# Moving z to token rows off TensorE: VectorE block transposes and sixteen SBUF-to-SBUF DMAs per sequence in a retention block plus expert layer

## The reference

```python
def block(h, p):
    r = _retention(h, wk)                  # scores q k^T, causal, divided by a row norm and a row sum, times v
    m = r @ w1 + b1
    a, gate = jnp.split(m, 2, axis=-1)
    m = a * jax.nn.silu(gate) @ w2 + b2    # "out projection"
    m = _groupnorm1(m, gg, gb)             # over a whole sequence
    y = m + h
    f = jax.nn.gelu(y @ wf1 + bf1_, approximate=False) @ wf2 + bf2_
    return (_layernorm(f + y, lg, lb), None)   # z = f + y; mean and variance over the 256 features of a token
out, _ = jax.lax.scan(block, x, params)    # 4 layers
x = _layernorm(x + out); x = _layernorm(x + _L0_ffn_ref(x, ...))   # 8 experts, hidden width 1024
```

## Time and profile before

| | |
|---|---|
| median of 3 runs | 2432.38 us (2432.0 to 2432.49) |
| the profiled execution, its own time | 2433.66 us |
| its span in the trace | 2431.9 us |
| TensorE busy | 2403.9 us, 99% of the span |
| VectorE / ScalarE / GpSimd busy | 1547.7 (64%) / 1366.8 (56%) / 1357.4 (56%) us |
| granted TensorE clock, mean | 0.996 of full |

### The profile page before, as it was taken

One profiled execution on the slowest core, in us unless ns is written; L12 is line 12 of the kernel. 1 busy time (PEld: TensorE's weight loads), 2 busy tenths in 40 slices (PEclk: granted clock), 3 DMA queues, 4 the chain that ended last, 5 costly groups with the idle time before them and its releaser, 6 DMA issues. The chain is left out here.

```text
span 2431.9 us, 35189 instructions
## 1 busy us (share of the span) xinstructions
PE 2403.9 (99%) x11662; PEld 2010.3 (83%) x11662; DVE 1547.7 (64%) x2876; ACT 1366.8 (56%) x2402; POOL 1357.4 (56%) x1255
## 2 busy tenths in 40 slices
PE   8999999999999999999999999999999999999998
PEld 6888888888888888887888888888888888888886
DVE  3566666666666666768787856665646756464545
ACT  4666766667666666666655644444444444444443
POOL 2355654455544644667888955546645556554444
PEclk9999999999999999999999999999999999999999
DMA  7011121111100112127655554544445443444442
GB/s 249 29 52 43 35 78 35 34 35 36 62 23 26 36 44 70 36 83 237 237 196 191 195 207 156 186 152 149 148 169 186 160 152 138 156 155 169 152 161 74
DMA packets 106823, 287.64 MB, mean 118 GB/s; under 512 B 7361, under 2 KB 77249, under 8 KB 90305
## 3 DMA queue, kind: packets, MB, share of 16 engines
q1 hardware_dynamic: 106128, 285.69, 33.7%
q10 hardware_dynamic: 560, 0.30, 0.0%
HBM read 216.36 MB, written 69.60 MB: 118 GB/s over the span
## 5 line engine op out<-in xcount | busy, mean ns | idle before, releaser
L701 POOL TENSOR_TENSOR hid_lo<-full,hid_hi 128x512 fp32r<-128x512 f32 x384 | 505.1, 1330 | 513.6 <-ACT full L1000 461.4
L1496 DVE SCALAR_TENSOR_TENSOR full<-ps,bias_cols,sum 128x512 f32<-128x512 f32 x384 | 288.2, 750 | 217.2 <-PE ps L1777 198.4
L1775 PE MATMUL ps<-hid_hi,m_w 128*128 128x512 f32 x1024 | 401.8, 392 | 0.1
L1777 PE MATMUL ps<-hid_hi,m_w 128*128 128x512 f32 x1024 | 398.8, 389 | 0.0
L1776 PE MATMUL ps<-hid_lo,m_w 128*128 128x512 f32 x1024 | 398.5, 389 | 0.0
L997 ACT ACTIVATE hid_hi<-ps,bias_cols 128x512 fp32r<-128x512 f32 x128 | 88.3, 690 | 496.4 <-PE ps L1777 496.4
L1775 PE MATMUL ps<-te_hi,m_w 128*128 128x512 f32 x896 | 351.5, 392 | 1.8 <-DVE sum L1483 0.9
L1777 PE MATMUL ps<-te_hi,m_w 128*128 128x512 f32 x896 | 349.3, 390 | 0.0
L1776 PE MATMUL ps<-te_lo,m_w 128*128 128x512 f32 x896 | 348.9, 389 | 0.0
L1777 PEld LDWEIGHTS ps<-hid_hi,m_w 128*128 128x128 f32 x1024 | 192.2, 188 | 40.4
L1775 PEld LDWEIGHTS ps<-hid_hi,m_w 128*128 128x128 f32 x1024 | 192.3, 188 | 39.5 <-issue 0.5
(11 more groups left out here) (210 smaller groups left out, 5593.2 us busy)
## 6 DMA issues: line engine op xcount, KB each, us to landing
m_w<-prepared SPq DMA_DIRECT2D x96, 1408.0 KB, 5.9
prepared<-m_w SPq DMA_DIRECT2D x32, 1408.0 KB, 5.8
h_store<-h_out SPq DMA_DIRECT2D x32, 512.0 KB, 3.2
we_raw<-in_W SPq DMA_DIRECT2D x64, 256.0 KB, 6.4
gate_bc<-gate_rows SPq DMA_DIRECT2D x64, 256.0 KB, 6.2
h_in<-h_store SPq DMA_DIRECT2D x24, 512.0 KB, 4.3
hT_in<-in_xT SPq DMA_DIRECT2D x8, 512.0 KB, 3.7
h_in<-in_x SPq DMA_DIRECT2D x8, 512.0 KB, 4.9
```

The source lines that it names most:

```text
L701: nc.gpsimd.tensor_tensor(out=hid_lo[:, k, :], in0=full[:, k, :], in1=f32(hid_hi[:, k, :]), op=ALU.subtract).then_inc(hid_ready, 1)
L1496: nc.vector.scalar_tensor_tensor(out=full[:, k, :], in0=src, scalar=b1_col(e, 2 * fp + BLOCK_ROW[k]), in1=other[:, :], op0=ALU.add, op1=AL ...
L1775: nc.tensor.matmul(out, w[0], x[0], start=first, stop=False, skip_group_check=True)
L1777: return nc.tensor.matmul(out, w[1], x[0], start=False, stop=last, skip_group_check=True)
```

## The change

For the first 15 steps' `z` (30 sequences) the eight PE transposes and the two ACT copies go. In their place:

- DVE turns each chunk of `z` by 32x32 blocks with `nc.vector.transpose` (`turn_z`) into the first half of the slot's `tmp` tile: four calls a step. Slot A's two stand inside `gated_products(B_, before)`, after each `gated`; slot B's first stands after `residual(B_, before, 0)`, its second inside `groupnorm_out(A_, now)`, ahead of `low_y` of chunk 0.
- SP then issues sixteen DMAs a sequence (`move_z`), each from a quadrant of 32 partitions of `tmp` to one of `z`: 32 rows x 8 pieces x 32 numbers, that is 32 KB in 256 pieces of 128 bytes. They stand ahead of the next loads of `h` for slot A, and between the loads and the store for slot B. `load_h` waits for its store first.
- `layernorm_stats` waits for all sixteen (`z_moved`), and so does the next `gated` of the slot, which overwrites `tmp`. Slot B's stats and var now stand after the two `divide(B_)`.
- `out_projection` goes over the input chunk `k` outside and the output chunk `c` inside, so that it needs the second chunk of its operand after six matmuls in place of three.
- `scores(B_)` goes chunk by chunk: blocks 0, 2, 3 with chunk 0, then block 0 with chunk 1, block 1, and blocks 2, 3 with chunk 1. Blocks 2 and 3 wait for the residuals that read their banks, no longer for `keep_z`.

The last step's two `z` keep the PE transposes. The core of the diff (renamed semaphores and the ends left out):

```diff
+        def turned_z(s):
+            return tmp[s][:, 0:DC, :].rearrange("p c n -> p (c n)").rearrange("p (r n b) -> p r n b", r=P // BLOCK, b=BLOCK)
+
+        def z_blocks(s, q, r):
+            rows = z[s][r * BLOCK:(r + 1) * BLOCK, :, :].rearrange("p k (c q b) -> p q (k c) b", c=DC, b=BLOCK)
+            return rows[:, q]
...
+            def move_z(s, it):
+
+                sp.wait_ge(h_new[s], it * U + U)
+                sp.wait_ge(z_ready[s], it * U + U)
+                for q in range(P // BLOCK):
+                    for r in range(P // BLOCK):
+                        sp.dma_start(z_blocks(s, q, r), turned_z(s)[q * BLOCK:(q + 1) * BLOCK, r, :, :]).then_inc(z_moved[s], DMA)
...
+                move_z(A_, it - 1)
+                load_next(A_)
+                move_z(B_, it - 1)
+                finish(A_)
+                load_next(B_)
+                finish(B_)
...
+            move_z(A_, STEPS - 2)
             sp.wait_ge(m2_psum[A_], DONE)
             load_weights(0)
             sp.wait_ge(y_ready[A_], DONE)
             load_weights(1)
+            move_z(B_, STEPS - 2)
             store_h(A_, STEPS - 2)
...
             def gated(s, at, c):
+                if c == 0:
+                    dve.wait_ge(z_moved[s], at.it * Z_MOVE + Z_STORE)
...
+            def turn_z(s, at, c):
+
+                dve.wait_ge(z_ready[s], at.base + residuals(s, c))
+                nc.vector.transpose(turned_z(s).rearrange("p r (k c) b -> p c k r b", c=DC)[:, c],
+                                    y[s][:, c, :].rearrange("p (k r b) -> p k r b", r=P // BLOCK, b=BLOCK)).then_inc(z_ready[s], 1)
...
-                    gated_products(B_, before)
+                    gated_products(B_, before, lambda part: turn_z(A_, before, part))
...
                     residual(B_, before, 0)
+                    turn_z(B_, before, 0)
...
-                groupnorm_out(A_, now)
+                groupnorm_out(A_, now, lambda part: before and part == 0 and turn_z(B_, before, 1))
                 low_p(B_, now, range(TB))
+                for half in range(2):
+                    divide(B_, now, half)
                 if before:
                     for blocks in HALVES:
                         layernorm_stats(B_, before, blocks)
                     layernorm_var(B_, before)
-                for half in range(2):
-                    divide(B_, now, half)
...
+            def scores_by_chunk(s, at, before):
+
+                for b in (0, 2, 3):
+                    score(s, at, b, 0, before)
+                score(s, at, 0, 1, before)
+                scores(s, at, (1,), before)
+                for b in (2, 3):
+                    score(s, at, b, 1, before)
...
-                for c in range(DC):
-                    for k in range(DC):
-                        pe.wait_ge(u_lo[s], at.base + 2 * k + 2)
+                for k in range(DC):
+                    pe.wait_ge(u_lo[s], at.base + 2 * k + 2)
+                    for c in range(DC):
                         ins = mm3(bank(s, OUT[c]), both(w, ALL, k, cols(c)), both(tu_sp[s], ALL, k), k == 0, k == DC - 1)
...
                 for c in range(DC):
                     project_t(A_, now, c)
                 if before:
-                    transpose_z(A_, before)
                     out_projection(B_, before)
...
                 group_moments(A_, now)
-                if before:
-                    transpose_z(B_, before)
-                else:
+                if not before:
                     pe.wait_ge(fold_out, 3 * (L - 1))
-                scores(B_, now, range(TB))
+                scores_by_chunk(B_, now, before)
```

More of the change, by code:

```diff
@@ L28 @@
 P = 128
+BLOCK = 32
 EPS = 1e-5
@@ L917, in hidden, with keep_z_end @@
                     high_f(s, at, c - 1)
-            def keep_z(s, at):
-                act.wait_ge(h_new[s], at.base + U)
+            def keep_z_end(s):
+                if s == A_:
+                    act.wait_ge(h_new[A_], LAST_STEP.base + U)
+                at_z, first = (z[A_], 0) if s == A_ else (z_end, 2)
                 for i in range(2):
[L922 to L930, removed]
+                    act.wait_ge(zT_psum, U * s + 2 * i + 2)
+                    nc.scalar.activation(at_z[:, 2 * i:2 * i + 2, :].rearrange("p k d -> p (k d)"), bank(s, first + i),
+                                         ACT.Copy).then_inc(z_kept, 2)
             def normalise_z(s, at, at_z=None):
@@ L1078, in body @@
                 high_t(B_, now)
-                if before:
-                    keep_z(B_, before)
-                else:
+                if not before:
                     act.wait_ge(fold_stored, (L - 1) * DMA)
@@ L1836, in project_t, with score, scores @@
                 ins.then_inc(t_psum[s], 2)
-            def scores(s, at, blocks):
+            def score(s, at, b, k, before):
+                q = slice(LO[b], S)
+                if k == 0 and b >= 2 and before:
+                    pe.wait_ge(z_ready[s], before.base + residuals(s, b - 2))
+                pe.wait_ge(t_lo[s], at.base + 2 * k + 2)
+                ins = mm3(score_bank(s, b)[:, q], both(hT_sp[s], ALL, k, cols(b)), both(tu_sp[s], ALL, k, q), k == 0, k == DC - 1)
+                if k == DC - 1:
+                    ins.then_inc(s_psum[s], 1)
+            def scores(s, at, blocks, before):
                 for b in blocks:
-                    q = slice(LO[b], S)
-                    if b == 2:
-                        pe.wait_ge(z_kept[s], at.base + U)
                     for k in range(DC):
-                        pe.wait_ge(t_lo[s], at.base + 2 * k + 2)
-                        ins = mm3(score_bank(s, b)[:, q], both(hT_sp[s], ALL, k, cols(b)), both(tu_sp[s], ALL, k, q),
-                                  k == 0, k == DC - 1)
-                    ins.then_inc(s_psum[s], 1)
+                        score(s, at, b, k, before)
+            def scores_by_chunk(s, at, before):
[5 more added lines that the diff above has]
+                    score(s, at, b, 1, before)
             def retain(s, at):
@@ L1879, in out_projection @@
                 w = weight("m2", DC)
-                pe.wait_ge(w_lo, split_count("m2", at.layer))
-                for c in range(DC):
-                    for k in range(DC):
-                        pe.wait_ge(u_lo[s], at.base + 2 * k + 2)
-                        ins = mm3(bank(s, OUT[c]), both(w, ALL, k, cols(c)), both(tu_sp[s], ALL, k), k == 0, k == DC - 1)
-                    ins.then_inc(m2_psum[s], 2)
-            def out_projection_end():
-                w = weight("m2", DC)
-                for k in range(DC):
-                    pe.wait_ge(u_lo[B_], LAST_STEP.base + 2 * k + 2)
-                    for c in range(DC):
-                        ins = mm3(bank(B_, OUT[c]), both(w, ALL, k, cols(c)), both(tu_sp[B_], ALL, k), k == 0, k == DC - 1)
+                if at is not LAST_STEP:
+                    pe.wait_ge(w_lo, split_count("m2", at.layer))
+                for k in range(DC):
+                    pe.wait_ge(u_lo[s], at.base + 2 * k + 2)
+                    for c in range(DC):
+                        ins = mm3(bank(s, OUT[c]), both(w, ALL, k, cols(c)), both(tu_sp[s], ALL, k), k == 0, k == DC - 1)
                         if k == DC - 1:
-                            ins.then_inc(m2_psum[B_], 2)
+                            ins.then_inc(m2_psum[s], 2)
             def down_projection_end():
@@ L2061, in body @@
                     fold_vm(0)
-                scores(A_, now, (0, 1))
+                scores(A_, now, (0, 1), before)
                 if before:
                     group_moments(B_, before)
-                scores(A_, now, (2, 3))
+                scores(A_, now, (2, 3), before)
                 if not before:
```

37 lines of the change are left out of this document (21 added, 16 removed).

## The result

| | before | after |
|---|---|---|
| median of the runs | 2432.19 us (2430.04 to 2432.49, 4 runs) | 2457.11 us (2456.15 to 2460.49, 4 runs) |
| span of the profiled execution | 2431.9 us | 2458.8 us |
| granted TensorE clock, mean | 0.996 | 0.993 |

The changed kernel takes 1.0107 times as long, 95% interval 1.0095 to 1.0119: 24.9 us slower. The forecast was 2429.6, "no change, slightly on the fast side", and the range ended at 2456. The forecast was wrong, and the time lies just outside its range.

A forecast was written before the change was run, and what follows sets the result against it. PE, busy 99% of the span, was taken to bound the kernel. Terms - 12.9 + 6.1 + 4.0 = - 2.8 us gave 2430.9 for the profiled execution, so a median of 2429.6; the 8-in-10 range was 2419 to 2456.

The forecast's parts named there:

- What bounds the kernel: Whole kernel: PE, busy 2403.9 of 2431.9 us, sets the time; DVE's low_u, low_t and the group norm stand directly behind.
- Slot A's 12.9 us: Slot A's out projection: removing PE's transposes wins 0.86 us in each of 15 steps, with u's second half still in time.
- rival 3: Slot A's low_u: DVE waits for GpSimd's passes if z lands early, PE waits at the out projection; 2447 us, chance 0.15.
- 0.7 us per transpose: DVE's new transposes: each taken at 0.7 us, after DVE's 128x512 passes of 0.69 to 0.75 us.
- Slot B, + 6.1 us: Slot A's y chain: slot B's transpose ahead of low_y delays PE by 0.41 us a step, 15 times; nothing won.
- The transfers, "hidden in 14 of 15 steps": Slot B's DMAs: landed at 655.7, DVE waits 0.5 us, low_r is not delayed, POOL's root starts 1.7 us later.
- The bound for small pieces: Slot B's DMAs, upper bound: if small pieces take as long as large, a sequence takes 16.9 us, landing near 665.
- The last body, + 4.0: Last body: slot B's transfers land at 1047.4, delaying the first expert tokens; PE waits about 4.0 us, not regained.
- Rival 2: Slot B's layer norm: transfers land late and push low_r; 2450 us at 4 us late, 2520 at worst; chance 0.17.

The follow-up runs named there:

- e3_both: Changed kernel with slot B's second transpose right behind its residual and, in the last body, first expert tokens normalised ahead of slot B's layer norm statistics: 2432.88 us, 1.0004.
- e2_x1_first: Changed kernel with one edit: in the last body DVE normalises the first expert tokens ahead of slot B's layer norm statistics; 2452.39 us, 1.0089.
- experiment 1: Changed kernel with slot B's second transpose moved from inside the group norm's output to right behind its residual; 2439.47 us, 1.0031.

## Why the prediction was wrong, point by point

- **What bounds the kernel**: right. PE at 99%, with its suppliers just in time. It is why an average of 64% on DVE was no comfort.
- **Slot A's 12.9 us**: the block is worth 0.86 us, and DVE's transposes are free in their gap, as forecast. The step that failed is "that half is wanted after six matmuls, 604.52 + 6 x 0.24 = 606.0, so it is in time by 0.7 us". It took the end of `low_u`, 605.28, from a step in which POOL's passes stood elsewhere. With the passes 3.2 us later the end is 606.16: late, by rival 3's mechanism, and the group norm's input behind it is late too. In sum, between the first mark and the last but one the forecast had - 12.9 + 6.1 = - 6.8 us, and + 19.0 were measured.
- **0.7 us per transpose**: right. The group has

```profile
L1352 DVE STREAM_TRANSPOSE tmp<-y 128x512 f32<-128x512 f32 x60 | 42.1, 702 | 0.5
```

The Trainium skill's 58 cycles plus one per number (VectorE: DVE Perf Modes, The TRN2 errata), by my estimate 594 ns, is 0.11 us short here. The same section says of this row that it under-predicts single operations and that the fixed term is nearer 150 cycles, which the prediction left out; by my estimate that is 690 ns for 512 numbers. The measured 702 ns decides.

- **Slot B, + 6.1 us**: the place and sign were right, the size not. In nine of eleven ordinary steps before, the last `low_y` ended 7.46 to 7.58 us behind the moments; the one that the forecast read was one of the two with 7.81 and 7.83. In the changed kernel it is 7.79 in all, so the chain moved by 0.2 to 0.3 in most and by nothing in those two. PE is through with its up projection 0.2 to 0.3 us later in most steps, some 3 to 4 us over the run by my estimate from these ends. With the transpose out of the chain (e3_both) it ends at 7.46 again behind the first layer.
- **The transfers, "hidden in 14 of 15 steps"**: this is the term that was mis-sized. The first issue came at 657.27 - 12.45 = 644.82, forecast 645.25. The sixteenth was to start at 652.8 and started at 667.1 - 12.45 = 654.65, because two issues of this kind start 0.65 us apart, not 0.50 as the two plain ones of the earlier trace rows. It landed 2.0 us later at 656.6, not 655.7. DVE waited 1.8 us for it, forecast 0.5. With statistics done at 658.8 and POOL's root at 658.98, POOL was 3.1 us late, forecast 1.7 on a start moved by 0.4. `low_r` started at 671.19 - 12.45 = 658.74, 0.24 us later than before: hardly pushed, as forecast.
- **The bound for small pieces** (16.9 us for a sequence) is far off: 256 pieces of 128 bytes land in 2.0 us, and the issuing queue, at 0.61 us each, sets the pace. The Trainium skill calls transfers under 64 KB dominated by descriptors (DMA: Bandwidth & Descriptors, Bandwidth); the late end that the prediction drew from it did not come. That page's exemption of SBUF-to-SBUF copies (Why small descriptors are slow) agrees with the 2.0 us.
- **The last body, + 4.0**: the mechanism was right. The wait was 5.3 us, because the sixteen issues took 11.2 us there and the transfers landed at 1067.2 - 17.6 = 1049.6, forecast 1047.4. What was not in the sum is what comes behind it. The granted clock, the third number from the end, of three stretches of the changed kernel:

```profile
1060.00:1080.00 20.00, 14.23 (x69) 11.68 (x68) 12.32 (x28) 8.27 (x15) 11.36 (x10) 0.83 0.18 42
1080.00:1100.00 20.00, 18.90 (x91) 16.14 (x90) 16.50 (x31) 12.16 (x20) 7.33 (x6) 0.80 0.30 99
1100.00:1120.00 20.00, 19.81 (x85) 15.49 (x85) 10.18 (x12) 11.44 (x19) 16.86 (x16) 0.95 0.29 99
```

and of the one stretch of the kernel before in which it fell:

```profile
1060.00:1080.00 20.00, 18.97 (x79) 16.14 (x79) 12.04 (x27) 11.30 (x19) 9.51 (x8) 0.74 0.23 72
```

Taken against full speed these are 8.4 us lost in 60, against 5.2. The transposes behind the idle PE take twice their time:

```profile
1064.36 1.03 PE L1913 MATMUL ps<-ident,y 128*128 128x128 f32 x8
1070.74 1.97 PE L2053 MATMUL ps<-ident,m_xs 128*128 128x128 f32 x8 [5.34 <-DVE m_xs L1405]
```

That is the lower of the two levels, 1.2 GHz, after 5.3 us in which PE did nothing. The edit of e2_x1_first took the idle time away, and the first of these stretches had its full clock again; the fall came one stretch later, at 0.74, the value it had before the change.

- **Rival 2** was right that transfers land late, wrong about what it would do: `low_r` was not pushed, the time went through POOL. **Rival 3**, at 0.15 and 2447 us, was the mechanism of the result: it had `low_u` end at 603.85 and 606.6, and they ended at 603.35 and 606.16. But I had tied it to z landing early, and it came of z landing late; I had taken the two rivals as alternatives where one causes the other. And I priced it from one ordinary step. The first layer, where the low half of hT has two SBUF operands as well, and the first and last changes of layers had no price of their own, and they are 18 us of the 26.9. The low clock behind PE's waits was in no term either: 7.0 us of those 18, and 3.2 more in the last body and behind it (8.4 less 5.2).

The forecast itself moved POOL's passes by 1.7 us and then read `low_u` as if they had not moved. With passes of 2.4 us back to back over the whole stretch in which both low halves are due, that step of the working needed an account of its own.

## What to carry to other kernels

- When a change moves the start of a chain on GpSimd, do not ask only who waits for the chain's end. Write down every VectorE pass with two SBUF operands in the stretch that the chain now covers, and ask which of the two will start first; a difference of 0.1 us decides over a whole pass. Splitting GpSimd's passes in two won some 9 us here once the rest was early, about 3 us with slot A alone, and nothing in the kernel before, where it shortened one pass of VectorE and lengthened the next.
- Price a train of DMAs by the spacing of DMAs of the same form and not of the nearest two that happen to follow each other, and turn, copy or otherwise finish the data as early as an idle gap on the producing engine allows: moving one transpose 5 us ahead into such a gap was worth 18 us.
- Read a slack from several steps: the one read here was one of the two smallest of eleven.
- Look at the granted clock of the stretch behind each new wait. Three waits of about 2 us were each followed here by 1.8 to 3.4 us lost to a low clock.

## What the runs showed of the hardware that I had not expected

- **DVE and POOL block each other, it is a race, and both sides can lose it.** DVE 0.09 us behind POOL's start: 2.85 us for a pass of 0.69. DVE 0.03 us ahead: 0.69, and POOL's pass 2.92 for 2.40 (experiment 1). The rule of the Trainium skill (SBUF — State Buffer, SBUF: two separate sides) that the first to start holds the ports for its whole instruction agrees with all of these rows.
- **Steps of the same code go by turns.** In experiment 1 ordinary steps won 1.3 us and lost 0.5, mostly by turns. That a step that gains brings DVE's pass to the other side of POOL's in the next one is what I take for the reason; no run tried it apart.
- **DVE's 32x32 block transposes are not held by POOL**: 60 of them took 0.69 to 0.71 us, also those that ran beside a long POOL pass (612.52 beside L409 of 610.44 to 612.86).
- **A pass with one operand can be held too.** The TENSOR_SCALAR of the earlier trace rows, four numbers a partition, took 1.20 us at 651.00 and ended 0.02 us after a POOL pass of 650.88 to 652.18. It did so in all fifteen steps in the kernel before, and took 0.17 us in all fifteen in the changed kernel, where POOL was waiting.
- **A SBUF-to-SBUF DMA of 256 pieces of 128 bytes** costs its queue 0.61 us and lands 2.0 us after its issue; a store of 512 KB lands after 3.2. The time went on the issuing side here, not on the moving side; that it is the number of pieces that makes an issue longer was not tried apart.
